# A layernorm centred and weighted by a product on TensorE, and a new order of the stages within a tick

## What is computed

```python
x = x + rwkv_model(layernorm(x))   # layernorm (ln0) on the normalised x, then 4 layers
for l in range(4):                 # inside rwkv_model, after x = layernorm(x, ln0_w, ln0_b)
    h = layernorm(x, ln1_w[l], ln1_b[l]); hh = shifted by one token
    k, v, r = products of mixes of h and hh with Wk, Wv, Wr
    x = x + (sigmoid(r) * wkv(decay, first, k, v)) @ Wo[l].T      # wkv: a scan over the tokens
    h = layernorm(x, ln2_w[l], ln2_b[l]); mixes as above
    x = x + sigmoid(xr @ Wcr.T) * (square(relu(xk @ Wck.T)) @ Wcv.T)
x = x + fp4_ffn(layernorm(x))      # gate, up, down with values rounded in blocks of 16
x = x + causal_attention(layernorm(x))
x = x + fp4_ffn(layernorm(x))
```

## Time and profile before

| what | value |
|---|---|
| median of 3 runs | 1402.53 us (1402.32 to 1403.51) |
| profiled execution, its own time | 1405.89 us |
| its span from first to last instruction | 1404.6 us |
| granted TensorE clock, mean | 0.988 |

### The profile page before, as it was taken

The page is one execution under the profiler, slowest core; times in us unless marked ns, Lnnn a source line. Parts: engine busy times, 40 slices in busy tenths (PEclk is TensorE's granted clock), DMA queues, the critical chain, the costliest instruction groups (busy, mean ns, idle before and its releaser), DMA issues.

```text
span 1404.6 us, 23693 instructions
## 1 busy us (share of the span) xinstructions
PE 1317.1 (94%) x7285; PEld 935.9 (67%) x7285; DVE 1263.4 (90%) x2169; ACT 1253.0 (89%) x2525; POOL 1163.5 (83%) x1218
## 2 busy tenths in 40 slices
PE   3789999999999999999999999989999999889996
PEld 1335667666666676676666766767677888667775
DVE  6999999999999999999999998569998666699994
ACT  6789999999999999999999998977778888968864
POOL 5888999999899899999998898879998534478974
PEclk9899999999999999999999999999999999999999
DMA  7000000001000000000000000010000000001011
GB/s 231 0 1 1 1 1 1 1 1 33 1 1 1 1 1 1 1 1 1 1 1 1 1 1 16 23 32 23 16 1 1 1 1 2 1 9 31 24 31 31
DMA packets 26925, 18.56 MB, mean 13 GB/s; under 512 B 1072, under 2 KB 26160, under 8 KB 26800
## 3 DMA queue, kind: packets, MB, share of 16 engines
q1 hardware_dynamic: 26800, 17.05, 4.1%
HBM read 12.85 MB, written 4.19 MB: 12 GB/s over the span
## 4 chain that ended last, share of the span: by engine, by line
PE 66%; DVE 17%; issue 7%; POOL 5%; ACT 5%; DMA 0%; SPq 0%; DVEq 0%; ACTq 0%; POOLq 0%
PE ps L1152 15%; PE ps L1135 14%; PE ps L1040 4%; PE ps L1142 4%; PE ps L1122 3%; PE ps L1105 3%; PE ps L1092 3%; PE ps L1093 3%; PE ps L1085 3%; PE ps L1261 2%; PE ps L1211 2%; PE ps L1243 2%; DVE ham L256 2%; DVE W L463 2%; POOL W L713 2%
## 5 line engine op out<-in xcount | busy, mean ns | idle before, releaser
L1152 PEld LDWEIGHTS ps<-W,kf 128*128 128x128 f32 x2048 | 245.2, 193 | 32.4 <-issue 30.2
L1135 PE MATMUL ps<-xk,W 128*128 128x512 f32 x512 | 264.2, 598 | 1.4 <-DVE W L463 1.4
L1152 PE MATMUL ps<-W,kf 128*128 128x128 f32 x2048 | 250.8, 276 | 0.8 <-DVE W L494 0.8
L757 ACT ACTIVATE z<-X,ln_rs 128x128 f32<-128x128 f32 x512 | 233.1, 669 | 3.1 <-POOL ln_rs L606 3.1
L867 ACT ACTIVATE kf<-ps 128x512 f32<-128x512 f32 x256 | 196.2, 766 | 4.1 <-PE ps L1135 4.1
L874 ACT ACTIVATE kf<-kf 128x1024 f32<-128x1024 f32 x128 | 158.2, 1236 | 0.0
L1040 PEld LDWEIGHTS ps<-idn,z 128*128 128x128 f32 x664 | 80.5, 142 | 100.1 <-issue 61.1
L1040 PE MATMUL ps<-idn,z 128*128 128x128 f32 x664 | 102.0, 277 | 44.0 <-DVE aa L366 21.1
L1135 PEld LDWEIGHTS ps<-xk,W 128*128 128x128 f32 x512 | 87.3, 192 | 59.0 <-issue 56.7
L604 POOL TENSOR_TENSOR ln_rs<-ln_rs,mhalf 128x8 f32<-128x8 f32 (+1 forms) x70 | 124.9, 1784 | 0.0
L713 POOL TENSOR_TENSOR W<-W,hsc 128x704 f32<-128x704 f32 x64 | 88.7, 1386 | 41.4 <-DVE W L494 41.2
(11 more groups left out here) (178 smaller groups left out, 3977.7 us busy)
## 6 DMA issues: line engine op xcount, KB each, us to landing
X<-x_in SPq DMA_DIRECT2D x16, 256.0 KB, 6.9
xi<-x_in SPq DMA_DIRECT2D x16, 256.0 KB, 2.9
out<-X SPq DMA_DIRECT2D x16, 256.0 KB, 2.3
W<-weights SPq DMA_DIRECT2D x4, 832.0 KB, 8.4
W<-fp4w SPq DMA_DIRECT2D x1, 560.0 KB, 3.7
row<-rows SPq DMA_DIRECT2D x1, 192.0 KB, 2.9
wqkv<-qkv SPq DMA_DIRECT2D x1, 96.0 KB, 5.9
idn<-ident SPq DMA_DIRECT2D x1, 64.0 KB, 3.6
```

The lines of the kernel that those rows point to most:

```text
L757: last = e.activation(chunk(dst, j), chunk(src, j), ACT.Identity, bias=rs[:, 1, j:j + 1], scale=rs[:, 0, j:j + 1])
L1135: e.matmul((pF0, pF1)[f % 2][:, :], w_of(r, WCK + f), xk[r % 2][:, :], start=True, stop=True).then_inc(kf_mm[f], 1)
L1152: last = e.matmul(chunk(pKV, j), kf[r % 3][:, f, j * 128:(j + 1) * 128], w_of(r, WCV + f), start=f == 0 and j == 0, stop=f == 3, skip_grou ...
```

## The change

Two things are changed together.

The first layernorm. Before, ACT centred and scaled each 128-token piece of X into `xi`, and DVE multiplied by `ln0_w` and added `ln0_b` (rows of `row`). Now PE turns X (`init_turn`, four transposes), ACT copies the turned tile to `xi` (`init_x`, one ACTIVATE of 128x512), PE multiplies it with a matrix `centre` = (identity − 1/128) · ln0_w that DVE makes once (`init_mm`, four products of 128 columns), and DVE scales each of four pieces by its inverse deviation and adds `ln0_b` in one SCALAR_TENSOR_TENSOR from PSUM. Statistics and `init_rsqrt` stay.

```diff
-                    w.wait_ge(small_here, 48)
-                    w.wait_ge(n_in.z, b + 1)
-                    e.tensor_tensor(by_tok(iz[b % 2]), by_tok(iz[b % 2]), to_toks(0), ALU.mult).then_inc(in_w, 1)
-                    w.wait_ge(in_w, b + 1)
-                    e.tensor_tensor(by_tok(X[b]), by_tok(iz[b % 2]), to_toks(1), ALU.add).then_inc(in_x, 1)
+                    rs = n_in.of(n_in.rs, b)
+                    w.wait_ge(n_in.nr, b + 1)
+                    w.wait_ge(in_mm, b + 1)
+                    for j in range(NT):
+                        last = e.scalar_tensor_tensor(out=chunk(X[b], j), in0=chunk(pR, j), scalar=rs[:, 0, j:j + 1],
+                                                      in1=row[:, 1, :], op0=ALU.mult, op1=ALU.add)
+                    last.then_inc(in_x, 1)
...
-            def init_z(b):
+            def init_x(b):
                 if 0 <= b < NB:
-                    w.wait_ge(in_x, b - 1)
-                    normalise(n_in, b, X[b], iz[b % 2])
+                    w.wait_ge(in_mm, b - 1)
+                    w.wait_ge(in_t, b + 1)
+                    e.activation(iz[b % 2][:, :], pT[:, :], ACT.Copy).then_inc(in_c, 1)
...
+            def init_turn(b):
+                if 0 <= b < NB:
+                    w.wait_ge(small_here, 48)
+                    w.wait_ge(x_here[b if b < 4 else 3 + b // 4], 16 if b < 4 else 64)
+                    w.wait_ge(*bT.hand_over(in_c, b + 1))
+                    turn(pT, X[b], in_t)
+
+            def init_mm(b):
+                if 0 <= b < NB:
+                    w.wait_ge(centre_done, 1)
+                    w.wait_ge(*bR.hand_over(in_x, b + 1))
+                    w.wait_ge(in_c, b + 1)
+                    for j in range(NT):
+                        last = e.matmul(chunk(pR, j), chunk(iz[b % 2], j), centre, start=True, stop=True)
+                    last.then_inc(in_mm, 1)
```

```diff
-Q_AT = 55
-FFN_AT = NR + 4
+Q_AT = 48
+FFN_AT = NR + 5
...
-                keys(t - 5)
+                keys(t - 6)
...
-                a_add(att_job(t - 8))
+                a_add(att_job(t - 6))
```

More of the change, by code:

```diff
@@ L546, in vector @@
[L546 to L559, removed]
@@ new lines, in vector @@
+                bn1(t - 3)
+                mul_up(ffn_job(t - 6), 1)
+                fx_sub(ffn_job(t - 4))
+                a_add(att_job(t - 6))
+                gate(t - 14)
+                fx_max(ffn_job(t - 2))
+                mul_rv(t - 7)
+                mul_up(ffn_job(t - 6), 2)
+                fh_add(ffn_job(t - 7), 0)
+                mul_up(ffn_job(t - 6), 3)
+                add_xa(t - 9)
+                mul_s1(t - 7)
+                fh_sub(ffn_job(t - 7), 0)
+                fh_max(ffn_job(t - 6))
@@ new lines, in scalar @@
+                keep_av(att_job(t - 5))
+                keep_hq(ffn_job(t - 8), 0)
+                exp_d(t - 7)
+                silu(ffn_job(t - 5), 0)
+                fh_magic(ffn_job(t - 7), 1)
+                relu(t - 13, 3)
+                keep_hq(ffn_job(t - 8), 1)
+                keep_x(ffn_job(t - 9))
+                norm2(t - 10)
+                keep_ax(att_job(t - 3))
+                relu(t - 12, 0)
+                square_1(t - 8)
+                tanh_r(t - 7)
+                a_exp(att_job(t - 4), 0)
@@ new lines, in tensor @@
+                lend_Y(ffn_job(t - 9))
+                a_values(att_job(t - 5))
+                output(t - 9)
+                f_gate(ffn_job(t - 6), 3)
+                f_up(ffn_job(t - 6), 3)
+                h_turn(ffn_job(t - 8), 0)
+                similarity(att_job(t - 4), 0)
+                f_gate(ffn_job(t - 5), 0)
+                h_turn(ffn_job(t - 8), 1)
+                down(ffn_job(t - 9))
+                lend_T(t - 7)
+                lend_M(ffn_job(t - 7), 1)
+                ff_keys(t - 13, 3)
@@ new lines, in tensor @@
+                a_turn(att_job(t - 3))
+                similarity(att_job(t - 4), 1)
+                receptance(t - 7)
+                h_turn(ffn_job(t - 8), 2)
+                ff_keys(t - 12, 0)
+                keys(t - 6)
+                ff_values(t - 13, 0)
+                p_turn(att_job(t - 5), 1)
+                ff_keys(t - 12, 1)
+                turn2(t - 10)
+                lend_O(t - 8)
+                similarity(att_job(t - 4), 2)
+                p_turn(att_job(t - 5), 2)
+                ff_gate(t - 13)
@@ new lines, in tensor @@
+                similarity(att_job(t - 4), 3)
+                ff_keys(t - 12, 2)
+                p_turn(att_job(t - 5), 3)
+                a_keys(att_job(t - 3))
+                f_up(ffn_job(t - 5), 0)
+                f_turn(ffn_job(t - 4))
+                lend_X(ffn_job(t - 3))
+                f_gate(ffn_job(t - 5), 1)
+                init_turn(t)
+                init_mm(t - 2)
+                f_up(ffn_job(t - 5), 1)
+                weights_in(t - Q_AT - 14)
+                ff_values(t - 13, 1)
```

231 lines of the change are left out of this document (94 added, 137 removed).

## The result

The changed kernel takes 1409.11 us in the median of 4 runs (1405.6 to 1410.55), the kernel before 1402.64 beside it: a ratio of 1.0038, 95% interval 1.0024 to 1.0052. It is slower by 0.4%. The forecast was 1405 with the range 1394 to 1415, and the most likely of the three signs was slower. The profiled execution took 1410.55 with a span of 1409.2; against the profiled execution of before that is 4.6 more of span. The difference of the medians is 6.5, because the profiled execution of before took 3.4 more than its kernel's first median and that of the change 1.4 more than its own. So the size of the difference may be somewhat smaller than 6.5; that was not measured.

The account below looks back on a forecast made before the run. It took PE and ACT to bound full RWKV ticks at 13.1 to 13.2 us, DVE the second FFN, PE attention. Terms −8 + 0 + 7 + 3 − 1 + 1 = +2 on the 1402.5 median gave 1404.5, stated as 1405, range 1394 to 1415.

Parts of the forecast that it names:

- the three signs: Whole kernel against a 2.8 us threshold: faster by more 0.33, within it 0.26, slower by more 0.41.
- Term 1: Fill at the start, ticks 0 to 17: −8 us, with the scan of tick 18 at 186.6 instead of 194.7.
- Term 2: Turning the fp4 weights, now tick 62: 0, costing 7 us there and no longer 7 in tick 69; −2 to +3.
- Term 3: From RWKV to the first FFN, ticks 67 to 76: +7 us from PE's load per tick, bounds +4 to +10.
- Term 4: First FFN into attention into second FFN, ticks 84 to 107: +3 us, bounds −3 to +8.
- Term 5: Second FFN: −1 us, 0.1 in each of 13 ticks, with DVE's sum of 9.9 unchanged; bounds −4 to +2.
- term 6: The end, `down` of job 30 now behind two turns of job 31 on PE: +1 us, bounds −2 to +3.
- PE's new work is hidden in the fill: Rival for ticks 13 to 17 and the overlaps: PE catches up, terms 1 and 4 −12 and −1, 1396 us; chance 0.30.
- A new wait in the full RWKV tick: Rival: some stage waits for another engine in 49 full ticks, 0.1 us each being 5 us; 1411 us, chance 0.19.

Follow-up runs that it names:

- the double product: The changed kernel with the centring product of `init_mm` issued twice per sequence, nothing else changed: 1413.81 us, ratio 1.0074 to the kernel before.

## Why the prediction was right, and where it was not

**Term 1, the fill, −8.** It held: −6.9 at tick 18, −6.2 at tick 54, and the double product shows the mechanism that the term was built on. The scan of tick 18 was forecast for 186.6 and stands at 187.8, but two errors partly cancel in that. Job 0's scan, in tick 6, came at 32.6 and not 29.9: the turn of X4 starts at 18.9, near my 18.6, but then PE waits 0.69, 0.93 and 0.69 us for ACT's copies between the pieces, and I had put these waits at nothing. The twelve ticks behind it took 155.2 us and not 156.7. The PE sum of 16.2 us was right for two intervals (16.2 and 15.8 up to the scans of ticks 15 and 16), but I had given it to three ticks; the five intervals up to tick 18 take 75.4 us, my five sums 78.1. I also costed the two parts only in their sum. Alone, the lists give −12 and the layernorm +5 to +6.

**Term 2, the weights, 0.** That tick 62 or 69 costs the same was right for the new lists (176.9 against 177.0). That it cost 7 in the old ones was wrong: spreading them there gives about 2.6 us in the profile, by the comparison above all of it the clock, and nothing that the median shows. The stretch of 78 us against 72 us of PE work in the earlier trace rows, from which I took that it was on the path, had slack in it. So the move was no exchange of 7 for 7: it cost 4.5 us up to tick 63, of which 3.2 are the clock in this profile, and tick 69 gave no 7 back (the difference is −0.9 at tick 68 and −0.8 at tick 75).

**Term 3, RWKV to the first FFN, +7.** From tick 54 to tick 81 the difference goes from −6.2 to +2.7: terms 2 and 3 are +8.9 together. By the marks 4.5 of them stand at ticks 62 and 63 and 4.7 at ticks 76 and 77. The sum of PE's loads gave about the right size, but it does not say why tick 77 takes 15.9 us. The timeline of PE does:

```profile
943.73 1.13 PE L1159 MATMUL ps<-xk,W 128*128 128x512 f32 x2 [0.25 <-DVE W L469]
947.80 3.40 PE L1176 MATMUL ps<-W,kf 128*128 128x128 f32 x16 [2.95 <-DVE W L500]
950.99 1.38 PE L1166 MATMUL ps<-W,xc 128*128 128x128 f32 x8
```

`ff_values` of a last RWKV job waits 2.95 us for the rounding of the first FFN job (L500), and behind that wait the clock is at its lower level again, 3.2 us for sixteen products. In the run with the weights over four ticks the wait is the same but the clock held, and tick 77 took 14.2 us; in the run without table loads the clock stayed low for longer, and it took 17.1.

**Term 4, the overlaps, +3.** The difference goes from +2.7 at tick 81 to +8.9 at tick 107 and +6.4 at tick 109, so the term is +3.7. The net was right, its make-up was not. I gave ticks 89 and 90 24 us of PE and "2 to 3" for the short chains of ticks 89 to 91; they take 28.5. The wait of `silu` behind the softmax is a part I had not seen. By the Trainium skill's price of a table switch (ScalarE: Activation LUTs, "What ACT_TABLE_LOAD costs", about 2.66 us with a drain) two of them would by estimate be 5.3 us here; the trace does not agree: taking them out gave 2.1, and the rows behind a load start at its end.

**Term 5, −1, and term 6, +1.** From tick 109 to tick 122 the difference falls from +6.4 to +3.2, so term 5 is −3, within its bounds, but not for my reason: the full ticks take 10.0 us in both kernels, and the gain lies from tick 118 on, where the jobs run out (9.2 us instead of 10.8 in that tick). The end adds 1.4, as forecast.

**The rivals.** "PE's new work is hidden in the fill" was to be decided by the scan of tick 18 under 183; it came at 187.8 and the double product cost its full 0.89 in each of ticks 12 to 18. "A new wait in the full RWKV tick" is excluded by 13.19.

**The sum** was +2 and the profiles say −6.2 + 8.9 + 3.7 − 3.2 + 1.4 = +4.6, the medians +6.5. The 2.6 between that and my sum are +1.8 in term 1 (at tick 54), +1.9 in terms 2 and 3, +0.7 in term 4, −2.2 in term 5 and +0.4 in term 6: the payback was larger and the gain of the fill smaller than forecast, each by some 2 us. The 1.9 between the profiles' +4.6 and the medians' +6.5 is that the profiled execution of before was itself above its median; I can name only that its clock was low in two places (0.86 from 760 to 772 us, and behind the weights), and that executions of the new layernorm scatter more (below). The sign came out as the likeliest of three, at 0.41, and the size was three times my +2.

## What to carry to other kernels

Work that is moved from a waiting engine to another is free only in the ticks in which that other one waits: here a second copy of the product cost nothing up to tick 11 and its full 0.9 us in each tick from 12 to 18, so add up each engine by tick, not over the stage. Then read the order of the list where two stages meet, since a call behind another stage's calls (here `silu` behind four exponentials and a layernorm, with DVE idle for 3.4 us) makes waits that show in no sum. A one-off block in which two engines hand a bank back and forth is best cut into pieces that lie one to a tick: that gave back 5.8 us where the tick was full, 3.2 of them the clock, and nothing that the medians show where there was slack.

## What the runs showed of the hardware

The level of PE's clock after short waits is not the same in each execution of the same instructions. At the weights it fell in one profile and held in another (3.2 us). Behind the wait of 2.95 us in tick 77 it held in one profile (tick 77 took 14.2 us), fell in the changed kernel's (15.9) and stayed low for longer in a third (17.1). At the start of the program it rose at about 33 us in the changed kernel's profile, and before 28.5 in that of the run with the weights in tick 69, the transposes of one job taking 1.11 and 0.66 us. First the changed kernel, then that run:

```profile
27.93 1.11 PE L1047 MATMUL ps<-idn,z 128*128 128x128 f32 x4 [0.69 <-ACT xi L788]
28.84 1.91 PE L1105 MATMUL ps<-h,big 128*128 128x512 f32 x2
```

```profile
28.23 0.66 PE L1047 MATMUL ps<-idn,z 128*128 128x128 f32 x4 [0.69 <-ACT xi L788]
28.72 1.02 PE L1105 MATMUL ps<-h,big 128*128 128x512 f32 x2
```

The scan of tick 24 stands at 264.7 in that run and at 266.8 in the changed kernel, 2.1 us apart with the same instructions up to there. The runs with the new layernorm that had ten executions spread over 8.7 to 9.0 us, each with some near its lowest and most 4 to 9 us higher; the old layernorm in the new lists spread over 2.2 to 2.5 us, and the kernel before over 4.3 us in 25 executions. The start and the weights would explain up to 5 us of such a spread, and tick 77 up to 2.9 more, but whether they are what makes it was not shown, since no profile fell among the lowest executions. The weights can't be all of it: the run with four pieces, where nothing falls there, spreads over 8.7 us, and the old layernorm with the weights in one tick over 2.5. Nor is it told by the clock alone: the profiled execution with four pieces had the highest mean clock of its ten (0.995) and took 1403.53, while four others at 0.993 took 1398.0 to 1398.6. So a difference of 3 us between two of the kernels with the new layernorm is read from their marks here, not from their medians.
